# Two lookups for the small cell, one for the large, a sum one cell earlier, digits first, three one-hot buffers

## What is computed

```python
def lstm_last(x, Wx, Wh, b):
    def step(carry, xt):
        h, c = carry
        g = xt @ Wx + h @ Wh + b
        i, f, gg, o = jnp.split(g, 4, axis=-1)
        c = jax.nn.sigmoid(f) * c + jax.nn.sigmoid(i) * jnp.tanh(gg)
        h = jax.nn.sigmoid(o) * jnp.tanh(c)
        return ((h, c), None)
...
m_from = lstm_last(base_emb[from_seq], seq_Wx, seq_Wh, seq_b)
m_to = lstm_last(base_emb[to_seq], seq_Wx, seq_Wh, seq_b)
def enc(ne, fe, Wx, Wh, b, nums, fr):
    x = jnp.concatenate([ne[nums], fe[fr]], axis=-1)
    return lstm_last(x, Wx, Wh, b)
nwf = jax.vmap(enc)(nwf_num_emb[fm], nwf_freq_emb[fm], nwf_Wx[fm], nwf_Wh[fm], nwf_b[fm], nwf_numbers, nwf_freqs)
...
return jax.nn.relu(feats @ reduce_W + reduce_b)
```

## Time and profile before

| | us |
|---|---|
| median of 3 runs | 1712.02 |
| lowest and highest | 1709.75, 1712.13 |
| the profiled execution, its own time | 1714.94 |
| span of that execution | 1713.1 |

### The profile page before, as it was taken

The page is one execution under the profiler, slowest core; times in us unless marked ns, Lnnn a source line. Parts: engine busy times, 40 slices in busy tenths (PEclk is TensorE's granted clock), DMA queues, the critical chain, the costliest instruction groups (busy, mean ns, idle before and its releaser), DMA issues.

```text
span 1713.1 us, 57020 instructions
## 1 busy us (share of the span) xinstructions
PE 1610.2 (94%) x23780; PEld 619.1 (36%) x23780; DVE 1509.0 (88%) x1573; ACT 1314.0 (77%) x2011; POOL 955.3 (56%) x473
## 2 busy tenths in 40 slices
PE   3799999999999999999999999999999999999997
PEld 0233333333333333333333333333333333333334
DVE  6788988989988989988989988988988988988984
ACT  4577777877777877777877778877778877778874
POOL 1445666776666776666754444554444554444553
PEclk8899999999999999999999999999999999999999
DMA  8678789898889898889788789899889888788870
GB/s 285 223 253 261 248 263 276 264 276 271 256 268 284 250 284 260 270 264 284 251 287 262 260 263 277 260 275 267 273 265 280 256 277 274 256 267 273 248 241 24
DMA packets 165793, 444.19 MB, mean 259 GB/s; under 512 B 45728, under 2 KB 103584, under 8 KB 132640
## 3 DMA queue, kind: packets, MB, share of 16 engines
q1 hardware_dynamic: 162112, 439.63, 81.8%
q0 software_dynamic: 2560, 0.15, 0.6%
q10 hardware_dynamic: 864, 0.75, 0.1%
HBM read 423.42 MB, written 6.82 MB: 251 GB/s over the span
## 4 chain that ended last, share of the span: by engine, by line
PE 53%; DVE 17%; ACT 15%; issue 9%; POOL 2%; DVEq 0%; POOLq 0%; ACTq 0%
PE e_ps L479 16%; PE ab L619 11%; PE f_ps L619 9%; PE ab L511 7%; DVE kept L493 7%; ACT gate L673 5%; DVE f_ps L705 5%; DVE seq_c L710 4%; ACT f_ps L671 3%; PE ab L425 3%; ACT tanh_c L664 3%; PE ab L560 2%; POOL ig L697 2%; ACT f_ps L673 2%; PE ab L570 2%
## 5 line engine op out<-in xcount | busy, mean ns | idle before, releaser
L697 POOL TENSOR_TENSOR ig<-gate 128x1024 f32<-128x1024 f32 x192 | 411.9, 2145 | 696.3 <-ACT seq_x L432 293.7
L479 PE MATMUL e_ps<-hot,tab 128*32 128x512 bf16 x8448 | 527.5, 384 | 61.6 <-DVE kept L493 56.8
L493 DVE SCALAR_TENSOR_TENSOR kept<-high,cst,e_ps 128x1024 f32<-128x1024 uint8 x352 | 449.1, 1276 | 49.6 <-PE e_ps L479 43.8
L619 PE MATMUL ab<-seq_h,seq_wh 64*64 64x512 f32 x3024 | 401.2, 590 | 0.0
L479 PEld LDWEIGHTS e_ps<-hot,tab 128*32 128x32 bf16 x8448 | 214.0, 97 | 486.8 <-issue 342.7
L469 DVE TENSOR_SCALAR hot<-low,cst 128x4096 bf16<-128x4096 bf16 x256 | 320.6, 1281 | 13.2 <-PE e_ps L479 13.2
L731 POOL TENSOR_TENSOR seq_h<-gate,tanh_c 128x1024 f32<-128x1024 f32 x128 | 308.9, 2414 | 31.8 <-ACT tanh_c L664 31.6
L673 ACT ACTIVATE gate<-ab,nwf_bias 128x512 f32<-128x512 f32 (+2 forms) x384 | 188.4, 553 | 166.2 <-PE ab L570 103.0
L671 ACT ACTIVATE gate<-ab 128x1024 f32<-128x1024 f32 x256 | 262.5, 1026 | 17.6 <-PE ab L619 8.8
L664 ACT ACTIVATE tanh_c<-seq_c 64x512 f32<-64x512 f32 (+1 forms) x384 | 241.9, 630 | 29.8 <-POOL nwf_h L731 22.1
L664 ACT ACTIVATE gate<-ab 64x512 f32<-64x512 f32 (+1 forms) x384 | 228.5, 595 | 9.4
(11 more groups left out here) (99 smaller groups left out, 1809.1 us busy)
## 6 DMA issues: line engine op xcount, KB each, us to landing
low<-low_digits SPq DMA_DIRECT2D x256, 1024.0 KB
low<-low_bytes SPq DMA_DIRECT2D x96, 512.0 KB
tok<-seq_tokens SPq DMA_DIRECT2D x128, 384.0 KB
high<-high_digits SPq DMA_DIRECT2D x1408, 32.0 KB
nwf_hq<-nwf_h SPq DMA_DIRECT2D x62, 128.0 KB
raw<-in_indices SPq DMA_DIRECT2D x32, 176.0 KB
low_digits<-low_of SPq DMA_DIRECT2D x32, 88.0 KB, 3.2
nwf_hq<-nwf_h SPq DMA_DIRECT2D x62, 32.0 KB, 3.0
```

Source lines behind the costliest of these rows:

```text
L479: last = nc.tensor.matmul(e_ps[32 * g:32 * g + 32, i, :], tab[:, part, 2 * m + ty, :], hot[:, p % HOT_RING, g, i, :], start=(part == 0), s ...
L493: nc.vector.scalar_tensor_tensor(out=kept[:, p % KEPT_RING, :, :], in0=wanted, scalar=cst[:, C_HIGH:C_HIGH + 1], in1=e_ps[:, :, :], op0=AL ...
L619: last = nc.tensor.matmul(flat(bank)[to:to + 64, cols], lhs(rows, half, block), rhs(rows, block, a, b), start=start, stop=stop)
L697: nc.gpsimd.tensor_tensor(ig[:, cols], gates[0][:, n % 2, cols], gates[1][:, n % 2, cols], ALU.mult).then_inc(ig_ready, 1)
```

## The change

`_share` becomes 2, 2, 2, 2, 2, 1: the small cell looks up two pairs (4 and 5), the large one one pair (10). A sum whose last pair is the first one of a seq cell is made in that cell, after its second lookup (`LATE_AT`); in each round but the first that is the sum of pairs 5 to 8, in the fourth seq cell in place of the large cell. The large cell has no lookup ahead of its gates any more; the small cell has one lookup ahead of gate 0 and one between gates 1 and FORGET. On DVE a cell of the second recurrence now makes digits first (large cell), then the first compare, and only then keeps its first pair. `hot` gets three buffers, while compares stay two pairs ahead (`COMPARED`). `PACKED` goes from pairs 0, 1, 6 to pairs 1, 6, 7.

```diff
--- before.py
+++ after.py
@@ -73,24 +73,32 @@
 PAIRS_AT = [[] for _ in CELLS]
 
 SUMS_AT = [[] for _ in CELLS]
+
+LATE_AT = [[] for _ in CELLS]
 for _r in range(NWF_T):
     _j = NPAIRS * _r
-    _share = [2, 2, 2, 3, 2] if _r == 0 else [2, 2, 1, 2, 2, 2]
+    _share = [2, 2, 2, 3, 2] if _r == 0 else [2, 2, 2, 2, 2, 1]
     _first = NUMBER["seq", 2 * _r, 0]
     for _k, _n in enumerate(_share):
         PAIRS_AT[_first + _k] = list(range(_j, _j + _n))
         _j += _n
-        SUMS_AT[_first + _k + 1] += [(_r, i) for i, pairs in enumerate(SUM_PAIRS)
-                                     if _j - _n <= NPAIRS * _r + pairs[-1] < _j]
+        for _i, _pairs in enumerate(SUM_PAIRS):
+            _last = NPAIRS * _r + _pairs[-1]
+            if _last == _j - _n and CELLS[_first + _k][0] == "seq":
+                LATE_AT[_first + _k].append((_r, _i))
+            elif _j - _n <= _last < _j:
+                SUMS_AT[_first + _k + 1].append((_r, _i))
 
 FIRST_ROUNDS = 1
 ROUND_AT = {(0, 3)[_r - 1] if _r < 3 else NUMBER["nwf", _r - 2, 0]: _r for _r in range(FIRST_ROUNDS, NWF_T)}
 
-PACKED = (0, 1, 6)
+PACKED = (1, 6, 7)
 
 ROUND_AWAY = 3.0 * 2 ** 30
 AHEAD, X_RING = 2, 3
-LOW_RING, HIGH_RING, HOT_RING, KEPT_RING = 4, 5, 2, 5
+LOW_RING, HIGH_RING, HOT_RING, KEPT_RING = 4, 5, 3, 5
+
+COMPARED = 2
 
 
 def later_seq(n):
@@ -108,8 +116,9 @@
 USES = [("sx", _s) for _s in range(AHEAD)]
 for _n in range(NCELLS):
     _x = [("x", _r, _i) for _r, _i in SUMS_AT[_n]]
+    _late = [("x", _r, _i) for _r, _i in LATE_AT[_n]]
     if CELLS[_n][0] == "seq":
-        USES += [("gate", _n, 0), *_x, ("gate", _n, 1)]
+        USES += [("gate", _n, 0), *_x, ("gate", _n, 1), *_late]
         if later_seq(_n) is not None:
             USES.append(("sx", later_seq(_n)))
         USES.append(("gate", _n, 3))
@@ -513,8 +522,8 @@
                                             start=(ty == 0), stop=(ty == 1))
             last.then_inc(ab_ready, 1)
 
-        def sums(pe, n):
-            for r, i in SUMS_AT[n]:
+        def sums(pe, those):
+            for r, i in those:
                 sum_up(pe, r, i)
 
         def store_x(act, r, i):
@@ -523,8 +532,8 @@
             act.wait_ge(ab_ready, USE[what] + 1)
             nc.scalar.copy(nwf_x[:, r % 2, at:at + cols], ab[USE[what] % 2][:, 0, 0:cols]).then_inc(ab_done, 1)
 
-        def store_sums(act, n):
-            for r, i in SUMS_AT[n]:
+        def store_sums(act, those):
+            for r, i in those:
                 store_x(act, r, i)
 
 
@@ -860,13 +869,20 @@
                 make_tables(dve)
                 for s in range(AHEAD):
                     seq_compare(dve, s)
-                for p in range(HOT_RING):
+                for p in range(COMPARED):
                     compare_pair(dve, p)
                 for n in range(NCELLS):
                     if n:
                         add_c(dve, n - 1)
                     pairs = PAIRS_AT[n]
-                    compared = [p + HOT_RING for p in pairs if p + HOT_RING < ALL_PAIRS]
+                    compared = [p + COMPARED for p in pairs if p + COMPARED < ALL_PAIRS]
+                    if CELLS[n][0] == "nwf":
+
+                        if n in ROUND_AT:
+                            make_digits(dve, ROUND_AT[n])
+                        for p in compared[:1]:
+                            compare_pair(dve, p)
+                        compared = compared[1:]
                     for p in pairs[:1]:
                         keep_wanted(dve, p)
                     if later_seq(n) is not None:
@@ -879,9 +895,6 @@
                         place_small_w(dve)
                     for p in compared[:2]:
                         compare_pair(dve, p)
-                        if p == compared[0] and n in ROUND_AT and CELLS[n][0] == "nwf":
-
-                            make_digits(dve, ROUND_AT[n])
                     for p in pairs[1:]:
                         keep_wanted(dve, p)
                     for p in compared[2:]:
@@ -915,7 +928,7 @@
                     if later_seq(n) is not None:
                         pool.wait_ge(seq_hot_ready, later_seq(n) + 1)
                     for p in PAIRS_AT[n][:2][-1:]:
-                        pool.wait_ge(hot_ready, min(p + HOT_RING + 1, ALL_PAIRS))
+                        pool.wait_ge(hot_ready, min(p + COMPARED + 1, ALL_PAIRS))
                     input_product(pool, n)
                     if FIRST_NWF < n < LAST:
                         new_h(pool, n - 1)
@@ -942,13 +955,14 @@
                     if n == LAST:
                         tanh_of(act, n - 1)
                     if not is_seq:
-                        store_sums(act, n)
+                        store_sums(act, SUMS_AT[n])
                     activate(act, n, 0)
                     if is_seq:
                         if n:
                             tanh_of(act, n - 1)
-                        store_sums(act, n)
+                        store_sums(act, SUMS_AT[n])
                     activate(act, n, 1)
+                    store_sums(act, LATE_AT[n])
                     if not is_seq and n < LAST:
                         tanh_of(act, n - 1)
                     if later_seq(n) is not None:
@@ -975,10 +989,11 @@
                         gate(pe, n, 0)
                         for p in pairs[:1]:
                             look_up(pe, p)
-                        sums(pe, n)
+                        sums(pe, SUMS_AT[n])
                     else:
-                        sums(pe, n)
-                        for p in pairs[:1]:
+                        sums(pe, SUMS_AT[n])
+
+                        for p in pairs[:-1]:
                             look_up(pe, p)
                         if not large:
                             gate(pe, n, 0)
@@ -986,8 +1001,9 @@
                         gates_of_large(pe, n, 0, 1)
                     else:
                         gate(pe, n, 1)
-                    for p in pairs[1:]:
+                    for p in pairs[1:] if CELLS[n][0] == "seq" else pairs[-1:]:
                         look_up(pe, p)
+                    sums(pe, LATE_AT[n])
                     if later_seq(n) is not None:
                         seq_lookup(pe, later_seq(n))
                     if large:
```

## The result

The changed kernel takes 1802.57 us (median of 4 runs, 1802.15 to 1804.14) against 1710.88 for the kernel before (4 runs, 1709.21 to 1712.13). The ratio is 1.0538, with a 95% interval of 1.052 to 1.0556: slower by 91.7 us. The prediction was 1807.6. The profiled execution of after took 1802.15, with a span of 1800.4 and a mean granted clock of 0.992 (before: span 1713.1, 0.989). Ratios and intervals in this document leave out executions over 1.5% slower than the fastest of their kernel, which are three of the ten in experiment 10 and none elsewhere.

What follows compares the result with a forecast made beforehand. Pace set by the forget-gate-to-second-lookup chain, with DVE slow in the large cell. Terms +93.3, +56.4, -58.6 and +4.5 gave +95.6 us on 1714.94, so 1810.5, median 1807.6; range 1765 to 1858, 8 in 10 and a little more.

Steps and rivals of the forecast that it cites:

- What bounds the kernel: Whole round: the chain from forget gate to second lookup sets the pace, not PE, though PE is busy 94%.
- Small cell: Between the forget gates around the small cell: 18.38 us against 15.37, +3.01 a round, the moved-in lookup waiting for the keep.
- The 0.6 for POOL: Small cell: the moved compare starts inside POOL's product and ends 0.6 us later; bounds 0 and 0.8.
- The sum: Fourth first-recurrence cell: the moved sum stands between second lookup and forget gate, +1.82 us a round.
- The 0.08 for one more change of weights: Fourth first-recurrence cell: estimated 0.08 us added to the sum's 1.74 for a weight change after the lookup.
- Large cell: From its preceding forget gate to the next round's second lookup: 15.90 us against 17.73, -1.83 a round.
- Rival A: Small and large cells: neither keep nor ab buffer delays PE, work only moves; -0.83 us a round, about 1683; chance 0.08.
- B: One wait absent: without the small cell's 1752 us, without the large gates' buffer wait 1744; chance 0.06.
- C: PE's clock falls after its waits in small and large cells, 1.3 to 2 us a round, 1858; chance 0.10.
- The extra 0.7 of the large gates: Large cell, rounds 2 to 14: gates take 0.7 us longer, on the path if it comes back; 4.5 taken, bounds 0 and 9.
- Round 1: Large cell of round 1: DVE's small tables come behind the keep, so the round gains 5.2 us.
- Round 30: Large cell of round 30: makes no digits, is 1.2 us shorter today, and gains 0.6 us.

Runs made afterwards that it cites:

- experiment 10: Kernel before with pair 6 alone packed, so the large cell's two compares are single ones; 1715.31 us, ratio 0.9998, runs 1698.97 to 1731.32.
- Experiment 1: Changed kernel, but in the small cell DVE keeps the first pair before it compares; 1759.47 us, ratio 1.0269.
- experiment 2: Changed kernel, but the sum of pairs 5 to 8 stands in the large cell again from round 1 on; 1777.14 us, ratio 1.0371.
- Experiment 5: Changed kernel, but the large cell issues its first two gates one after the other, not interleaved; 1797.32 us, ratio 1.0497.
- experiment 7: Kernel before, but from round 3 on the digits are made in the small cell, not the large one; 1803.11 us, ratio 1.0529.
- experiment 6: Changed kernel with the keep first in the small cell and the sum of pairs 5 to 8 back in the large cell; 1750.67 us, ratio 1.0218.
- experiment 4: Kernel before with three one-hot buffers in place of two, compares still two pairs ahead; 1713.08 us, ratio 1.0003.
- experiment 12: Kernel before with pairs 1, 6, 7 packed and three one-hot buffers, lookups, sums and order as before; 1701.5 us, ratio 0.9943.
- experiment 9: Changed kernel with keep first in the small cell, sum back in the large cell, and no POOL gather issued in large cells; 1744.01 us, ratio 1.0184.

## Why the prediction was right

**What bounds the kernel.** The reading held: the pace is that of the chain from forget gate to second lookup, and PE's busy share says little. Experiments 1, 2 and 5 moved the stretches in which they changed that chain or what stands ahead of it, and left the others.

**Small cell.** Forecast: second lookup at F1 + 8.98, after a wait of 1.8. Measured: 877.95 - 868.93 = 9.02, a wait of 1.62. The 0.6 for POOL was 0.72 (1.47 against 0.75). What follows the lookup took 9.24 where the sum had 9.40, so the stretch came to 18.24 and not 18.38. Experiment 1 shows the step itself: with the keep first the stretch is 16.85 and 43.1 us are gone.

The Trainium skill, page SBUF — State Buffer, section Who interferes with whom, says that the engine that comes second is blocked for the other's whole instruction. The runs agree to within 0.2 us: the halves of 0.74 and 1.27 ended 0.57 and 1.08 after POOL's product, the digit instruction of 0.25 (experiment 7) 0.12 after it.

**The sum.** Forecast 1.82, measured 1.72 (896.56 - 894.85 = 1.71 from the sum to the next matmul). The 0.08 for one more change of weights had no row behind it, and doesn't show.

**Large cell.** Forecast: gates begin at F3 + 2.2, go on at 4.27, lookup at 6.66, and 9.24 from there. Measured: 2.27, 4.28, 6.60 and 9.24. Rival A needed the buffer to be free by F3 + 2.2. ACT read it at F3 + 4.2, as forecast, and the keep of the small cell was late too, so both conditions of A and both cases of B fell. Experiment 5 takes the first gate's need for the buffer away, but its gates take 4.24 us in place of 2.42, so it doesn't say what the stretch would be with a free buffer alone. C fell as well: PE's granted clock in after has no dip between 120 and 1778 us.

**Terms that were mis-sized.** The extra 0.7 of the large gates in rounds 2 to 14, put in with 4.5 us of a possible 9, came to nothing: all rounds of after from 2 on but two show 17.68 (17.94 and 19.02 in the others). Round 1 was to gain 5.2 and gained 1.7 in F3 to F0 (22.95 to 21.25). DVE's small tables, which the change lets run behind the keep, met POOL's products there. DVE:

```profile
145.97 1.76 DVE L345 TENSOR_SCALAR few_f<-few_in 128x16 f32<-128x16 int32 x1
147.76 2.29 DVE L346 TENSOR_SCALAR few_idx<-few_f 128x16 int32<-128x16 f32 x1
...
150.29 0.18 DVE L345 TENSOR_SCALAR few_f<-few_in 128x32 f32<-128x32 int32 x1
```

and PE's lookup behind them, answering:

```profile
155.54 1.48 PE L488 MATMUL e_ps<-hot,tab 128*32 128x512 bf16 x24 [3.72 <-DVE kept L502]
```

Tiny instructions that take 0.18 took 1.76 and 2.29, held by POOL. I had used that rule for the one compare that the change moves and not for the tables it moves too. Round 30 was read as 1.2 us shorter; its F3 to F0 was 0.62 shorter (18.95), and it gained 1.3 in place of 0.6.

Over all rounds the two traces differ from the forecast like this:

| part | forecast | measured |
|---|---|---|
| small cell, rounds 1 to 31 | +93.3 | +91.1 |
| sum, rounds 1 to 31 | +56.4 | +53.0 |
| large cell, round 1 | -5.2 | -1.7 |
| large cell, rounds 2 to 29, with the 4.5 for the gates | -46.7 | -52.6 |
| large cell, round 30 | -0.6 | -1.3 |
| behind the last forget gate | -1.6 | -2.5 |
| start and round 0 | 0 | +1.2 |
| together | +95.6 | +87.2 |

The large cell of rounds 2 to 29 holds a pause of 1.3 us in round 29. The misses have both signs, so the total is closer than its parts. The median was missed by 5.0 us, of which 1.1 lies in the kernel before (1710.88 for 1712.02) and 3.9 in the difference (91.7 for 95.6). That this is less than the 8.4 of the traces is luck: it comes from which executions were profiled.

**Why the idea doesn't pay.** With the order of DVE and the place of the sum as they were (experiment 6), a lookup moved from the large cell to the small one costs 1.49 a round there (16.85 against 15.36) and brings at most 1.18 in the large one (19.57 to 18.39, rounds without a gather), for the gates then wait for ACT's copy of the sum. The compare ahead of the keep in the small cell and the sum in the fourth seq cell cost more than they free. The large cell's slowness was DVE's, and 0.6 us of it could be had by changing which pairs are packed. What digits and compare ahead of the keep do in the large cell was not tried by itself.

**Open.** Why the large gates stand still in their middle in rounds with gathers: 3.1 us in before and experiment 7, 3.65 in experiment 6. They take 2.42 to 2.45 in experiments 4, 10 and 12 and 2.5 in experiment 9, with a gather at the same distance from their start. Where they stand still, that ends with the last gather beside the gates (round 14), so gathers seem to have a part in it, but not by themselves.

## What to carry to other kernels

Before moving work to an engine with idle time, find the chain that sets the pace and ask whether the work lands ahead of a link of it; here DVE had time in the small cell, but a compare ahead of the keep cost 43 us and digits there cost 90. Where one engine's instructions hold up another's, as POOL's products do with DVE's here, list every instruction that a reordering brings beside the other engine's long ones, the tiny ones too. When an engine is late in one stretch, first try making its work there cheaper at the expense of a stretch where it has time: that was worth 0.57% at no change of order.

## What the runs showed of the hardware

- A DVE TENSOR_SCALAR that starts while POOL's product is running is held until that product is all but over: int16 to bf16 (1.47 against 0.74), uint8 to bf16 (1.97 against 1.27), int16 to int16 (2.31 against 0.25), int32 to int16 (1.28 against 0.34, 29 times in experiment 2), int32 to f32 (1.76 against 0.18). I had expected the byte form to be free. The keep, with PSUM among its inputs, takes 1.27 to 1.29 in every row shown.
- The other order holds POOL. In after DVE was inside a compare from 42.36 us on, with two more behind it that took their usual 1.27 or 1.28 each, when this product began. It took twice its usual 2.4 us:

```profile
42.90 4.80 POOL L740 TENSOR_TENSOR seq_h<-gate,tanh_c 128x1024 f32<-128x1024 f32 x1 [3.35 <-ACT tanh_c L673]
```

- PE's clock: the lookups after waits of 1.62 and 3.72 us in after took 1.48. After waits of 2.2 to 2.3 us (experiment 7) the lookup took 2.75, at 0.50 of the clock, in most rounds, and 1.48 in seven. What besides the wait decides it isn't shown.
- PE pauses of 0.6 to 2.0 us, 19 of 20 of them before 32x32 matmuls, end 2.3 to 2.8 us after a packet of the instruction queue. They fall on other rounds in other kernels, and the six in the profile of experiment 6 come to 7.5 us.
